# Sigmoid moved behind the arctangent, the half-gate products projected second and third, and a second buffer for the real part

## The reference

```
x = x + 0.5 * experts(layernorm(x))
x = x + attn(layernorm(x))
x = x + 0.5 * experts(layernorm(x))

attn(x):
    q, k, v, g = x@Wq, x@Wk, x@Wv, x@Wg
    a = x@Wa                  # real and imaginary halves
    a_c = sigmoid(|a|) * exp(1j * angle(a))
    h[t] = a_c[t] * h[t-1] + k[t]*v[t]        # along the sequence
    y = real((q * h * silu(g)) @ Wo)
    y = layer_norm(y + x)
    return layer_norm(gelu(y@W1 + b1)@W2 + b2 + y)
```

## Time and profile before

| what | value |
|---|---|
| median of 3 runs | 715.59 us (712.15 to 718.97) |
| the profiled execution's own time | 716.23 us |
| span of its trace | 714.5 us |
| TensorE busy | 660.4 us, 92% |
| VectorE busy | 479.2 us, 67% |
| ScalarE busy | 450.8 us, 63% |
| GpSimd busy | 195.3 us, 27% |

### The profile page before, as it was taken

The page is one execution under the profiler, slowest core; times in us unless marked ns, Lnnn a source line. Parts: engine busy times, 40 slices in busy tenths (PEclk is TensorE's granted clock), DMA queues, the critical chain, the costliest instruction groups (busy, mean ns, idle before and its releaser), DMA issues. The chain is left out here.

```text
span 714.5 us, 11765 instructions
## 1 busy us (share of the span) xinstructions
PE 660.4 (92%) x4412; PEld 572.8 (80%) x4425; DVE 479.2 (67%) x1059; ACT 450.8 (63%) x811; POOL 195.3 (27%) x290
## 2 busy tenths in 40 slices
PE   8888999999999899999999899999898999799993
PEld 5357999756659789798899799799787789589993
DVE  4671540155898989989989989988889877610001
ACT  3313444228869898888898898898698243344440
POOL 5231011221022124234234235234035131410112
PEclk9997999999999999999999999999999999799997
DMA  8985693061001201201210220111011086117700
GB/s 279 340 281 194 224 304 128 35 192 57 33 30 60 75 1 46 74 19 57 74 50 27 74 74 7 68 45 44 2 45 45 2 303 227 60 31 243 250 24 25
DMA packets 53009, 74.09 MB, mean 104 GB/s; under 512 B 4774, under 2 KB 44795, under 8 KB 52952
## 3 DMA queue, kind: packets, MB, share of 16 engines
q1 hardware_dynamic: 44376, 55.64, 24.0%
q0 software_dynamic: 4352, 13.49, 5.3%
q10 hardware_dynamic: 4224, 4.19, 1.7%
HBM read 58.26 MB, written 15.20 MB: 103 GB/s over the span
## 5 line engine op out<-in xcount | busy, mean ns | idle before, releaser
L993 PE MATMUL bank<-xdt,ring 128*128 128x160 f32 x512 | 78.7, 314 | 5.1 <-issue 3.3
L1650 PE MATMUL bank<-zt_h,w_in_h 128*128 128x512 f32 x192 | 78.9, 411 | 4.4 <-DVE qg L1324 1.6
L993 PEld LDWEIGHTS bank<-xdt,ring 128*128 128x128 f32 x512 | 75.5, 202 | 6.6 <-issue 6.6
L1650 PE MATMUL bank<-yt_h,w_h 128*128 128x256 f32 x256 | 73.6, 288 | 6.1 <-DVE yt_l L1434 3.9
L792 DVE SCALAR_TENSOR_TENSOR xo<-bank,gate,xg 128x256 f32<-128x256 f32 x20 | 9.2, 482 | 99.4 <-PE bank L1020 99.4
L1652 PE MATMUL bank<-zt_h,w_in_l 128*128 128x512 f32 x192 | 75.1, 391 | 0.0
L1651 PE MATMUL bank<-zt_l,w_in_h 128*128 128x512 f32 x192 | 75.0, 391 | 0.0
L1006 PE MATMUL bank<-hid,ring 128*128 128x160 f32 x512 | 72.8, 300 | 1.5 <-DVE idx_s L776 0.7
L1650 PE MATMUL bank<-w_h,ht_h 128*128 128x256 f32 x256 | 73.7, 288 | 0.0
L830 ACT ACTIVATE hid<-bank,b1t 128x160 f32<-128x160 f32 x128 | 50.1, 394 | 35.1 <-PE bank L993 11.7
L1006 PEld LDWEIGHTS bank<-hid,ring 128*128 128x128 f32 x512 | 70.4, 190 | 2.3 <-issue 2.3
(11 more groups left out here) (249 smaller groups left out, 1642.5 us busy)
## 6 DMA issues: line engine op xcount, KB each, us to landing
ring<-in_L_ffn_w SPq DMA_DIRECT2D x32, 1024.0 KB, 8.1
xc<-in_L_attn_x SPq DMA_DIRECT2D x8, 512.0 KB, 5.0
x_mid<-xc ACTq DMA_DIRECT2D x8, 512.0 KB, 6.4
z_mid<-zb POOLq DMA_DIRECT2D x8, 512.0 KB, 3.4
zr<-z_mid SPq DMA_DIRECT2D x16, 256.0 KB, 2.8
xr<-x_mid SPq DMA_DIRECT2D x16, 256.0 KB, 3.7
out<-xq POOLq DMA_DIRECT2D x16, 256.0 KB, 4.3
zb<-x_mid SPq DMA_DIRECT2D x7, 512.0 KB, 5.2
```

Source lines behind the costliest of these rows:

```text
L993: ins = T.matmul(bank[b][:, 0:CAP], w1_of(s)[:, k, m * P:(m + 1) * P], xdt[:, k, e * CAP:(e + 1) * CAP], start=k == 0, stop=k == KD - 1)
L1650: T.matmul(out, left[0], right[0], start=start, stop=False)
```

## The change

- A table `PARTS` names what each projection j is: real part of half 0, gate of half 0, gate of half 1, real part of half 1, k of half 0, k of half 1. So the two gate projections (g and q, with the Silu) are j = 1 and 2, and the two k projections j = 4 and 5. `project`, `read` and `fold` follow it.
- `gate_half` (Sigmoid) moves from before the feed-forward gelus (in the first two blocks: from behind `root`) to directly behind `phase` (Arctan). The one-column Silu moves from the end of `phase` to the end of `gate_half`.
- `gate` (VectorE) moves from behind the first `tangent` to behind `turns`.
- `re` gets a second buffer, by parity, allocated behind all other tiles; the read of the real part waits for the gate of two blocks back, no longer for that of the block before.
- All reads that fill `kv` and `qg` wait for `yo` of two blocks back. Nothing else moves: the filler matmuls, the transfers and the feed-forward steps stand where they stood.

```
+PARTS = ((0, RE), (0, GG), (1, GG), (1, RE), (0, KK), (1, KK))
...
 STEPS (the same moves in FIRST_STEPS and LAST_STEPS)
-    (0, "tangent", 0), (0, "gate_half", 0), (0, "gate", 0), (-1, "gelu", 0), (-1, "gelu", 1), (-1, "split", 0),
+    (0, "tangent", 0), (-1, "gelu", 0), (-1, "gelu", 1), (-1, "split", 0),
...
-    (0, "phase", 0), (1, "read", 1), (0, "rounding", 0), (-2, "next_turn", 1), (-1, "down", 0), (1, "fold", 1),
-    (-1, "mix_norm", 1), (-1, "mix_turn", 1), (0, "turns", 0), (-1, "out_stats", 0), (-1, "mix_split", 1),
+    (0, "phase", 0), (0, "gate_half", 0), (1, "read", 1),
+    (0, "rounding", 0), (-2, "next_turn", 1), (-1, "down", 0), (1, "fold", 1), (-1, "mix_norm", 1),
+    (-1, "mix_turn", 1), (0, "turns", 0), (0, "gate", 0), (-1, "out_stats", 0), (-1, "mix_split", 1),
...
-        re, im = sb("re", [P, KD, BT]), sb("im", [P, KD, BT])
+        re, im = [sb("re0", [P, KD, BT])], sb("im", [P, KD, BT])
...
+        re.append(sb("re1", [P, KD, BT]))
...
             def fold(b, j):
+                h, part = PARTS[j]
+                t = (kv if part == KK else qg)[b.par][:, h, :]
+                v.wait_ge(proj_read[0], b.n * 7 + (j + 2))
+                v.wait_ge(proj_ready[1], b.n * 7 + (j + 2))
+                V.tensor_tensor(t, t, proj[1][:], ALU.mult).then_inc(proj_read[1], 1)
...
             def read(b, j):
-                if i == 0:
-                    if later:
-                        wait(act, gate_done, b.n)
-                    S.activation(re[:, h, :], proj[0][:], ACT.Copy).then_inc(proj_read[0], 1)
+                if part == RE:
+                    wait(act, gate_done, b.n - 1)
+                    S.activation(re[b.par][:, h, :], proj[0][:], ACT.Copy).then_inc(proj_read[0], 1)
...
+                wait(act, yg_done, b.n * 2 - 2)
+                if part == KK:
                     S.activation(k, proj[0][:], ACT.Copy).then_inc(proj_read[0], 1)
-                if i == 2:
+                else:
                     S.activation(g, proj[0][:], ACT.Silu).then_inc(proj_read[0], 1)
...
             def gate_half(b, j):
                 act.wait_ge(rho, b.n * 2 + KD)
                 S.activation(tg[:], ta[:], ACT.Sigmoid).then_inc(half_ready, 1)
+                own.step(S.activation(spare[:, 0:1], tiny[:], ACT.Silu))
...
             def phase(b, j):
                 for h in range(KD):
                     act.wait_ge(t_done, b.n * 2 + (h + 1))
                     S.activation(tb[:, h, :], tb[:, h, :], ACT.Arctan, scale=-1.0).then_inc(angle, 1)
-                own.step(S.activation(spare[:, 0:1], tiny[:], ACT.Silu))
...
             def project(b, j):
+                h, part = PARTS[j]
                 for n in range(2):
+                    wait(pe, proj_read[n], b.n * 7 + (1 + j))
+                    c = slice((part + n) * D + h * P, (part + n) * D + (h + 1) * P)
```

More of the change, by code:

```diff
@@ L73 @@
[L73 to L87, removed]
+    (0, "busy", 7), (0, "z_low", 0), (0, "project", 0), (0, "read", 0), (1, "z_stats", 0), (0, "project", 1),
@@ new lines @@
+    (0, "phase", 0), (0, "gate_half", 0), (1, "read", 1), (1, "fold", 1), (0, "busy", 10), (1, "project", 2),
+    (0, "rounding", 0), (1, "read", 2), (0, "turns", 0), (0, "gate", 0), (1, "fold", 2), (0, "turned_back", 0),
+    (0, "scan", 0), (0, "scan", 1), (0, "rotate", 0), (0, "gated", 0), (0, "gated", 1), (1, "project", 3),
+    (1, "project", 4), (1, "read", 3), (0, "wo", 0), (1, "read", 4), (1, "fold", 4), (2, "z_norm", 0), (0, "back", 0),
+    (0, "load_quarter", 0), (1, "square", 0), (1, "size", 0), (1, "root", 0), (0, "mix_stats", 0), (1, "project", 5),
@@ L88 @@
+    (0, "split", 3), (0, "down", 0), (1, "phase", 0), (1, "gate_half", 0), (1, "rounding", 0), (2, "read", 1),
+    (2, "project", 2), (0, "mix_norm", 1), (1, "turns", 0), (1, "gate", 0), (2, "fold", 1), (0, "out_stats", 0),
+    (0, "out_norm", 0), (0, "mix_turn", 1), (0, "mix_split", 1), (0, "up", 4), (2, "read", 2), (1, "load_quarter", 0),
     (1, "load_quarter", 1),
@@ L92 @@
 STEPS = (
[L93 to L97, removed]
@@ L140 @@
[L140 to L144, removed]
@@ new lines @@
+    (-1, "fold", 1), (-3, "mix_norm", 1), (-3, "mix_turn", 1), (-2, "turns", 0), (-2, "gate", 0),
+    (-3, "out_stats", 0), (-3, "mix_split", 1), (-4, "logits", 1), (-1, "project", 2), (-1, "read", 2),
+    (-3, "out_norm", 0), (-3, "up", 4), (-3, "up", 5), (-2, "turned_back", 0), (-1, "fold", 2),
+    (-1, "load_quarter", 0), (-2, "scan", 0), (-1, "project", 3), (-2, "scan", 1), (-3, "gelu", 4), (-3, "gelu", 5),
+    (-3, "split", 4), (-2, "rotate", 0), (-3, "next_turn", 0), (-1, "read", 3), (-2, "back", 0), (-3, "split", 5),
@@ L151 @@
+    (-2, "mix_split", 0), (-2, "up", 0), (-2, "up", 1), (-3, "out_norm", 1), (-1, "tangent", 0), (-2, "gelu", 0),
     (-2, "gelu", 1), (-2, "split", 0), (-2, "split", 1), (-2, "up", 2), (-2, "up", 3), (-1, "tangent", 1),
     (-2, "gelu", 2), (-2, "split", 2), (-2, "gelu", 3), (-2, "split", 3), (-2, "mix_stats", 1), (-1, "phase", 0),
[L153 to L154 removed]
@@ L165 @@
[L165 to L169 removed]
+    (-1, "gate_half", 0), (-1, "rounding", 0), (-3, "next_turn", 1), (-2, "down", 0), (-2, "mix_norm", 1),
@@ new lines @@
+    (-1, "busy", 6), (-2, "mix_turn", 1), (-1, "turns", 0), (-1, "gate", 0), (-2, "out_stats", 0),
+    (-2, "mix_split", 1), (-3, "logits", 1), (-2, "out_norm", 0), (-1, "busy", 4), (-2, "up", 4), (-2, "up", 5),
+    (-1, "turned_back", 0), (-1, "scan", 0), (-1, "scan", 1), (-2, "gelu", 4), (-2, "gelu", 5), (-2, "split", 4),
+    (-1, "rotate", 0), (-2, "next_turn", 0), (-1, "back", 0), (-2, "split", 5), (-2, "up", 6), (-2, "up", 7),
+    (-1, "gated", 0), (-1, "gated", 1), (-2, "gelu", 6), (-2, "logits", 0), (-1, "busy", 27), (-1, "wo", 0),
```

127 lines of the change are left out of this document (57 added, 70 removed).

## The result

On the chip of the prediction the changed kernel took 725.52 us (median, 723.43 to 726.33, 4 runs) against 717.28 us (712.15 to 721.40, 4 runs): a ratio of 1.0111, interval 1.0067 to 1.0154. On a second chip it was 718.39 against 710.49, 1.0112 (1.0070 to 1.0154). It is slower by 1.1%, where 714.7 us (711 to 719), no difference, was forecast. The ratios in this text are worked out over the single runs and not from the two medians. The two differ by up to 0.3%, so differences of that size between kernels say little. Its profiled execution took 726.33 us, with a span of 724.6 against 714.5.

The account below looks back on a forecast made before the run. Bound: a loop of 18.8 us VectorE and 33 us TensorE, 51.8 a round. First two blocks -0.5, five rounds 0, last block -0.35: -0.85 from 716.23 gives 715.4; the median lies 0.64 lower, so 714.7 us (711 to 719).

Parts of the forecast that it names:

- The loads: ScalarE: 15 table loads of 1.283 us, 19.2 us over the run, go away; the Silu's are hidden, value 0 a round.
- The rival of two tables: Sigmoid and Arctan don't share a table, so a 1.28 us load stands between them: 723.0 us, chance 0.06.
- the loop shortened by a freed ScalarE: TensorE's wait for `yo`, up to 1.62 us, goes away in five rounds: 707.3 us, chance 0.09.
- Behind the arctangent: ScalarE: the 1.06 us Sigmoid comes before the Silu's load; the second rounding still ends at about 283.3, against 283.31.
- The VectorE term: Steady rounds: the 1.22 us gate moves behind `turns` and adds nothing; five rounds 0, from -2.1 to +2.3 us.
- So the gate fills the wait, with nothing over: VectorE behind `turns`: the gate ends at 285.24, when `down` ends and `out_stats` starts; value 0 a round.
- the 0.4 us ahead of it: VectorE ahead of the scan: without the gate there, the scan starts at 279.9 instead of 280.33.
- No transfer, filler or GpSimd step moves past another: From the paragraph on costs: the new order adds none through transfers, fillers or GpSimd steps.
- The gate lands on VectorE's loop: Rival: 0.4 us not gained or roundings later; rounds pay 0.4 to 0.5, ends 0.7 each: 719.3 us, chance 0.15.
- The sign for failure: The prediction is wrong if VectorE meets a wait between the new gate and `yo` that the old order lacked.
- The last block: The gate goes into VectorE's 1.00 us wait for ScalarE's turned quarter: -0.35 us, ends -0.8 and +0.7.
- The third rival: Freed ScalarE shortens the loop by removing the wait for `yo` in five rounds: 707.3 us, chance 0.09.

## Why the prediction was wrong

The forecast was 714.7 us, and 725.5 were measured. Of the 10.8 us between them 1.7 are the base: the kernel before came to 717.28 in the runs beside the change, against the 715.59 that the forecast started from. The rest is the change's own.

**The loads: right, and worth nothing.** 15 fewer, none ahead of Sigmoid or of `read` 5; the freed time became waits for TensorE (0.80 us ahead of a gelu). The projections alone gave 1.0021 with the interval over 1. The rival of two tables is out. So is that of the loop shortened by a freed ScalarE: TensorE's waits for `yo` grew, from 1.65 to 2.3 us in the longest of them.

**Behind the arctangent: right.** The Sigmoid took 1.04 us, and `turns` still started behind the fold with no wait for ScalarE. Block 0 gained 0.5 us, where 0.3 was forecast: from ScalarE's first read of its transposed input to its `yo` 50.55 us (154.41 to 204.96), against 51.06 before (150.65 to 201.71). The round to block 1 is 0.4 us shorter in the first profile and 0.5 us longer in the second.

**The VectorE term: the step that failed.** "So the gate fills the wait, with nothing over" priced the gate at the 1.22 us it has in its old place and looked at VectorE's queue alone. The order came out as forecast, to the point that `out_stats` starts right behind the gate. In the first profile the scan starts 29.0 us behind the `yo` before it in the rounds to blocks 3, 4 and 5, against 29.3 before, so 0.3 of the 0.4 us ahead of it were gained, and length alone costs about 0.1 us: in blocks 3 and 5, with a gate of 1.22, `out_stats` starts 34.3 us behind that `yo`, against 34.2 before. What had no place in the sum was GpSimd: in the new place the gate costs 2.31 us in even blocks and in odd ones holds a product for 2.13 us, which reaches `vn`, TensorE and VectorE. Measured: 1.0 to 1.5 us in the rounds to blocks 2 and 4 (52.77 against 51.77 in the second), 0.8 to 0.9 in those to 3 and 5 (52.68 and 52.74 against 51.86 and 51.87), and 0.7 in that to block 6, where `turns` is held, in place of 0. The cause is shown from three sides. The gate moved alone gives the long rounds to blocks 2 to 5; the add taken away gives the even rounds back, in the change only; and the add moved and the product left out give all of it back, where the kernel before loses or gains nothing by one column of add (1.0001) or by the missing product (0.9996). The two parts don't simply add: each engine's delay decides what it meets next, so that the product left out alone brought almost nothing.

**"No transfer, filler or GpSimd step moves past another": right in words, wrong in use.** GpSimd's own order is unchanged. But VectorE's gate moved beside GpSimd's second-quarter steps, and that was not looked at. The Trainium skill ("SBUF — State Buffer", SBUF: two separate sides, on the shared pair) says that a GpSimd operation and a VectorE operation with both inputs in that memory exclude each other, and that the one that comes second waits for the whole of the other. By that rule, the traces agree: 1.73 us of add begun 0.5 us ahead of the gate leaves it 1.2 us to wait, and it took 1.1 more; and an operation of one input and the same length left GpSimd's products at 0.39 and 0.99, and the add beside it at 1.73 and 1.27. By this page, and the trace's lengths, the gate's price could have been bounded: an estimate of 1.22 + 1.73 us at most.

**The rival that came closest.** "The gate lands on VectorE's loop" had the right place and rounds of 52.2 for its sign; they were 52.7 to 52.8. It blamed ScalarE or the 0.4 us ahead of the scan, and had no GpSimd in it, so that it has the right place is in part luck. Five rounds of 0.9 us are 4.5 us, where it had 2.3. The sign for failure that the text named, a wait of VectorE between the new gate and `yo`, is what block 3 shows.

**The last block: wrong.** The round to block 7 was to be 0.35 us shorter, and it took 52.15 and 50.92 against 49.80; its gate was held as well (2.29). The gate moved alone has 1.22 there and 49.68, and in the round to block 6 it has 51.83 against the change's 52.44 and 52.48. So in the two last rounds the whole change pays for GpSimd where the gate alone doesn't: 1.9 us, with the second profile's figures.

**A slip in the prediction.** The third rival's 707.3 us is counted from the profiled execution's 716.23, the other rivals' times from the median of 715.59. By the median it is 706.7. No chance hangs on it.

**What stays open.** The gate alone costs 0.52%, the whole change 1.11%, 4.2 us more. The two last rounds explain 1.9 of them. For the rest TensorE's clock is the candidate. The means of the granted clock over the runs were 0.964 for the change on the second chip, 0.967 with the add moved, and 0.974 both for the gate alone and with add and product out of the way, against 0.977 before. Within the runs of one kernel, 0.001 less of it goes with 0.49 us more (one slope fitted to all kernels, each with its own mean). The change's mean of 719.1 us is 8.6 above before's 710.6, and 0.0128 of clock at that rate is 6.3 of them, which overlaps with the stalls.

Three things on record speak against reading the slope as a cause. The kernel with fillers had a clock of 0.971, by the slope 3.4 us less than the change's, and its mean was 1.3 us less. The kernel with add and product out of the way lost nothing at 0.974, where the slope gives it 1 us. And kernels with the gate in its old place have low stretches too: five of their six profiles have one or two behind a `yo` in the rounds to blocks 2 to 6 (53.13 to 53.56 in place of 51.8). They have fewer: at 1.2 GHz these six spent some 7 to 14 us between 150 and 600 us, the two profiles of the change 24 and 27. That the stalls bring the low clock, and with it the rest of the loss, is possible and not shown.

## What to carry to other kernels

A free slot in one engine's order is free only if the engines it shares something with are idle in it too: before moving an operation, lay GpSimd's list beside VectorE's for the new place, and price it at its length plus the longest neighbour, for the moved operation and for those beside it. A GpSimd step of two columns can be the critical one, when an activation and a transposition hang on it. And freeing the engine that waits for others, here 20 us of ScalarE, buys nothing by itself.

## What the runs showed of the hardware

- A GpSimd product of two columns took 0.20 us at its shortest and 0.39 to 2.13 us beside VectorE operations with two inputs; the add of 512 columns 1.26 to 1.73 and up to 3.31. A VectorE operation with one input (1.21 us) lengthened neither.
- Either engine can be the one that is held: the gate (2.31 us) behind an add that had begun, the product (2.13) behind `turns` and the gate that had. Blocks of the same program fell on either side.
- Sigmoid and Arctan stand under one table (no load between 281.43 and 282.48 in the profile after), and so do Silu and Sin (8 loads at L1582 serve the one-column Silu and the sines of 8 blocks).
- TensorE's low-clock stretches of some 4 us (a few of 7) behind waits of 1.4 to 2.5 us are irregular: the two profiles of the changed kernel have them partly in different rounds, and many waits of 1.6 us have none behind them. Behind `yo` one costs 1.3 to 1.8 us; 37 us later in the round, nothing that shows.
